# Last stage of a three-stage image kernel: the normalisation of one image pair woven into the MLP of the pair before it, written out instruction by instruction on every engine

## The chip, the cores and the metric

One NeuronCore of a Trainium2 chip runs the whole program. The metric is device time in microseconds (us). One NeuronCore has a tensor engine (PE in the profile, with its weight loads as PEld), a vector engine (DVE), a scalar engine (ACT), GpSimd (POOL) and a sync engine (SP) that here only issues DMAs. Each engine works through its own instructions in order, and semaphores tie the engines together.

## The reference, cut to what matters

Three stages follow one another: an attention block, a 25-step non-negative factorisation (which leaves `h`), and the stage that this change touches. That last stage is, for 32 images of 96 channels by 32 x 32 pixels:

```
def layernorm_last(x, g, b):
    mu = x.mean(axis=-1, keepdims=True)
    var = ((x - mu) ** 2).mean(axis=-1, keepdims=True)
    return (x - mu) * lax.rsqrt(var + 1e-05) * g + b
...
x = x + nnmf_conv(jnp.maximum(x_norm, EPS), Wc)      # nnmf_conv returns h
y = x.transpose(0, 2, 3, 1)
yn = layernorm_last(y, g2, b2)
hid = jax.nn.gelu(yn @ w_fc1 + b_fc1, approximate=False)
y = y + (hid @ w_fc2 + b_fc2)
return y.transpose(0, 3, 1, 2)
```

The normalisation is over the 96 channels; the MLP goes from 96 to 384 and back to 96.

## The kernel before

Only the last stage, `token_mlp`, matters here. Channels lie on the partitions. The work goes by pairs of images, 16 pairs in all, and each pair has four units (`UNITS = 4`) of 96 channels by 512 pixels. The buffers carry the prefix `ml_` in the profile.

**Normalisation of a pair (`norm`).** SP loads `xt` (2 DMAs) and `ht` (8 DMAs) one pair ahead. ACT copies `ht` into pixel order, four `hn` copies (L1433). DVE adds them, `yt` (L1503), once for each image. Then for each unit: PE subtracts the mean by a float32 product with `centre` (`ml_PX`, L1558); ACT squares it (`ml_sqr`, L1440); PE averages over the channels (`ml_PV`, L1551); ACT takes Ln (`ml_vl`, L1447) and Exp (`ml_vy`, L1451); DVE refines the inverse root and scales in four steps, `ml_va`, `ml_vb`, `ml_vr`, `ml_yn` (L1507, L1509, L1511, L1515); ACT writes the float16 upper part `y16[0]` (L1466), and POOL the lower part `y16[1]` (L1408). `ml_PX`, `ml_PV`, `ml_sqr`, `ml_vy` and `ml_yn` are rings of two.

**MLP of a pair (`mlp`).** For each unit and each of three groups `m` of 128 hidden rows: PE multiplies in three float16 passes (`ml_PG`, L1578); ACT takes the gelu into `g32[m]` (L1475); DVE casts it to float16 (`g16[0]`, L1530); POOL subtracts to get the lower part (`g16[1]`, L1417). Then PE multiplies back with nine passes (`ml_PO`, one buffer, L1569), DVE adds bias and `yt` into `ml_ot` (L1523), and SP stores it (L1390). `g32` has three buffers, one for each `m`.

**Order.** `program` runs the same coarse order on every engine: the whole normalisation of pair b+1, then the whole MLP of pair b, and so on; a hardware loop over t holds two pairs. No engine starts the MLP's instructions before it has issued all of its normalisation instructions. ACT loads another function table at the start of each half (L1425, L1475).

Of the kernel before, what the change touches and what calls it, by code (L numbers as in the profile page):

```python
# [1285 lines left out]
UNITS = 4  # L1286


def token_mlp(nc, x2_dram, h_dram, g2, be2, wf1, bf1, wf2, bf2, out):
# [9 lines left out]
    with ctx:  # L1299
# [64 lines left out]
        @block.sync
        def _(e):
# [16 lines left out]
            def norm(b, p, early):  # L1382

                if not (isinstance(b, int) and b == B - 1):
                    load(b + 1, 1 - p, isinstance(b, int) and b == 0)

            def mlp(b, p, early):
                for u in range(UNITS):
                    e.wait_ge(s_out, UNITS * b + u + 1)
                    e.dma_start(out[bass.ds(2 * b + u // 2, 1), :, HALF * (u % 2):HALF * (u % 2) + HALF].rearrange("a c n -> (a c) n"),  # L1390
                                ot[u % 2][:, :]).then_inc(s_stored[u % 2], 16)
            load(0, 0, True)
            program(e, norm, mlp)
            for v in (0, 1):
                e.wait_ge(s_stored[v], 16 * NIMG)
# [23 lines left out]

        @block.scalar  # L1420
        def _(e):
            e.wait_ge(s_ready, 1)

            def norm(b, p, early):
                e.preload_act_table_set("natural_log_exp_and_others")  # L1425
                for v in (0, 1):
                    i = 2 * p + v
                    e.wait_ge(s_h_loaded[p], 64 * (b - p) + 128)
                    if not (isinstance(b, int) and b == 0):
                        e.wait_ge(s_y, 2 * b + v - 1)  # L1430
                    for y in (0, 1):

                        e.activation(hn[v][:, :].rearrange("c (r y k x) -> c y r k x", y=2, k=AC, x=PX)[:, y],  # L1433
                                     ht[p][:, :, y, :, :, v].rearrange("c x k r -> c r k x"), ACT.Copy, scale=1.0 / H_SCALE).then_inc(s_hn, 1)
                def square(u):
                    n = UNITS * b + u
                    e.wait_ge(s_centred, n + 1)
                    if not (isinstance(b, int) and b == 0 and u < 2):
                        e.wait_ge(s_var, n - 1)
                    e.activation(sqr[u % 2][:, :], PX_[u % 2][0:CH, :], ACT.Square).then_inc(s_sqr, 1)  # L1440

                def inverse_root(u):
                    n = UNITS * b + u
                    e.wait_ge(s_var, n + 1)
                    if not (isinstance(b, int) and b == 0 and u < 1):
                        e.wait_ge(s_vy, n)
                    e.activation(vl[:, :], PV[u % 2][0:CH, :], ACT.Ln, bias=eps_c[:, :]).then_inc(s_vl, 1)  # L1447
                    e.wait_ge(s_vl, n + 1)
                    if not (isinstance(b, int) and b == 0 and u < 2):
                        e.wait_ge(s_vr, n - 1)  # L1450
                    e.activation(vy[u % 2][:, :], vl[:, :], ACT.Exp, scale=-0.5).then_inc(s_vy, 1)  # L1451


                square(0); square(1)
                for u in range(0, UNITS, 2):
                    inverse_root(u); inverse_root(u + 1)
                    for v in (u, u + 1):
                        high(b, p, v, early)
                        if v + 2 < UNITS:
                            square(v + 2)  # L1460

            def high(b, p, u, early):
                e.wait_ge(s_yn, UNITS * b + u + 1)
                if not early:
                    e.wait_ge(s_fc1, 3 * (UNITS * (b - 2) + u) + 3)
                e.activation(y16[0][:, p, u, :], yn[u % 2][:, :], ACT.Copy).then_inc(s_yn_hi, 1)  # L1466

            def mlp(b, p, early):
                for u in range(UNITS):
                    for m in range(3):  # L1470
                        n = 3 * (UNITS * b + u) + m
# [139 lines left out]
```

## Time and profile before

| | |
|---|---|
| three runs, median (lowest to highest) | 7554.52 us (7553.3 to 7556.19) |
| profiled execution, its own time | 7552.64 us |
| its span, first to last instruction | 7550.9 us |
| mean granted TensorE clock | 0.956 |
| last stage, from about 6757 us to the end | about 794 us |
| busy in six pairs of the last stage, mean per pair | PE 30.4, DVE 26.8, ACT 24.6, POOL 19.9 us of 47.8 |

The windows of pairs run from one second-half centring to the next. Rows of a view give the start or the busy time first, then the engine, the line and the operation, with outputs to the left of the arrow; what stands in brackets is how long the engine had been idle and what ended the wait.

### The profile page before, as it was taken

Reading aid. Unit: us, or ns where it says so; the run is one execution under the profiler, and the core shown is the slowest. Engines: PE = TensorE matmul, PEld = TensorE weight load, DVE = VectorE, ACT = ScalarE, POOL = GpSimd, SP = SyncE. Lnnn points to the kernel's source line nnn. Section 1 sums busy time; section 2 is a strip of 40 time slices with the busy share of each in tenths; the row PEclk is TensorE's granted clock in tenths of the full one; section 3 lists DMA queues with packets and bytes.
Section 4 is the critical chain, followed back from the end, with each engine's and each line's share of the span. In section 5 each row is a group of like instructions: output and inputs, shape, how many; then the busy total and the mean of one; then the engine's idle time right before and its main releaser. Section 6 shows DMA issues by size and latency. Waiting matters only on the chain. (4 is left out here: it accounts for less than half of the span.)

```text
span 7550.9 us, 237789 instructions
## 1 busy us (share of the span) xinstructions
PE 6477.1 (86%) x97977; PEld 3568.9 (47%) x97977; DVE 5483.5 (73%) x8000; ACT 4590.7 (61%) x6901; POOL 4709.7 (62%) x3220
## 2 busy tenths in 40 slices
PE   7999999999588888888888878888878888866666
PEld 3444444444355555455555545555545555532222
DVE  5666666666588888778888868888868888865555
ACT  3444444444277777667777757777757777755554
POOL 3333333333188788768888767888767888863444
PEclk9999999999799999999999999999999999987778
DMA  0000000000100000000000010000010000011111
GB/s 15 20 22 24 17 24 20 22 24 16 37 3 3 3 3 3 31 11 3 3 3 3 3 39 3 3 3 3 3 39 3 3 3 3 3 45 38 50 50 38
DMA packets 92369, 119.74 MB, mean 16 GB/s; under 512 B 23696, under 2 KB 73136, under 8 KB 91568
## 3 DMA queue, kind: packets, MB, share of 16 engines
q1 hardware_dynamic: 91568, 106.87, 4.7%
q8 instruction: 770, 12.62, 0.7%
q14 instruction: 31, 0.25, 0.0%
HBM read 53.67 MB, written 52.79 MB: 14 GB/s over the span
## 5 line engine op out<-in xcount | busy, mean ns | idle before, releaser
L190 POOL TENSOR_TENSOR nn_hf<-nn_hf,nn_sr 128x512 f32<-128x512 f32 (+1 forms) x800 | 1444.3, 1828 | 807.7 <-DVE nn_sr L380 807.7
L464 PE MATMUL nn_P<-nn_hh,nn_w 64*64 64x256 f16 x38400 | 1565.2, 279 | 319.2 <-issue 86.9
L464 PEld LDWEIGHTS nn_P<-nn_hh,nn_w 64*64 64x64 f16 x38400 | 980.7, 108 | 1001.7 <-issue 948.3
L385 DVE SCALAR_TENSOR_TENSOR nn_P<-nn_P,nn_xs 128x612 f32<-128x612 f32 x1200 | 962.3, 802 | 546.9 <-PE nn_P L464 537.1
L471 PE MATMUL nn_P<-nn_nh,nn_w 64*64 64x512 f16 x19200 | 1276.1, 379 | 72.1 <-DVE nn_hf L371 9.3
L258 ACT ACTIVATE nn_yy<-nn_P 128x612 f32<-128x612 f32 x1200 | 810.2, 675 | 787.2 <-DVE nn_P L385 782.4
L1168 PE MATMUL at_PC<-at_xp,at_w1T 97*128 97x512 f16 x5184 | 1235.8, 383 | 0.0
L391 DVE TENSOR_TENSOR nn_P<-nn_P,nn_nh 128x612 f32<-128x612 f32 x1200 | 958.2, 798 | 123.7 <-ACT nn_nh L262 116.3
L396 DVE SCALAR_TENSOR_TENSOR nn_nl<-nn_P,nn_yy 128x612 f16<-128x612 f32 x1200 | 952.0, 793 | 88.4 <-ACT nn_yy L265 56.2
L464 PE MATMUL nn_P<-nn_hl,nn_w 64*64 64x256 f16 x19200 | 988.3, 274 | 0.0
L276 ACT ACTIVATE nn_hh<-nn_hf 128x512 f16<-128x512 f32 (+1 forms) x780 | 650.8, 834 | 523.9 <-POOL nn_hf L190 523.8
L371 DVE TENSOR_TENSOR nn_hf<-nn_P,nn_hf 128x512 f32<-128x512 f32 x1200 | 786.9, 684 | 136.6 <-PE nn_P L471 136.6
L262 ACT ACTIVATE nn_nh<-nn_yy 128x612 f16<-128x612 f32 x1200 | 856.3, 714 | 37.9
L184 POOL TENSOR_TENSOR nn_acc<-nn_acc,nn_hf 128x512 f32<-128x512 f32 x600 | 768.7, 1281 | 125.0 <-DVE nn_hf L371 124.6
L265 ACT ACTIVATE nn_yy<-nn_yy 128x612 f32<-128x612 f32 x1200 | 836.6, 697 | 0.0
L202 POOL TENSOR_TENSOR nn_hl<-nn_hf,nn_hh 128x1024 f16<-128x1024 f32 x384 | 823.5, 2144 | 0.0
L471 PEld LDWEIGHTS nn_P<-nn_nh,nn_w 64*64 64x64 f16 x19200 | 532.3, 105 | 592.2 <-issue 366.7
L1168 PEld LDWEIGHTS at_PC<-at_xp,at_w1T 97*128 97x128 f16 x5184 | 495.1, 97 | 657.8 <-issue 89.4
L471 PE MATMUL nn_P<-nn_nl,nn_w 64*64 64x512 f16 x9600 | 743.2, 375 | 0.0
L464 PEld LDWEIGHTS nn_P<-nn_hl,nn_w 64*64 64x64 f16 x19200 | 590.8, 109 | 4.5 <-issue 0.8
L194 POOL TENSOR_TENSOR nn_hl<-nn_hf,nn_hh 128x512 f16<-128x512 f32 x392 | 458.8, 1170 | 0.0
L505 PE MATMUL nn_PS<-nn_acc,nn_blk 128*128 128x512 f32 x400 | 226.1, 647 | 260.1 <-POOL nn_acc L184 260.1
(210 smaller groups left out, 7742.0 us busy)
## 6 DMA issues: line engine op xcount, KB each, us to landing
xn_scratch<-at_xb SPq DMA_DIRECT2D x128, 114.8 KB
nn_xs<-xn_scratch SPq DMA_DIRECT2D x48, 306.0 KB, 4.5
at_x<-in_x SPq DMA_DIRECT2D x32, 384.0 KB, 3.2
x_scratch<-at_x SPq DMA_DIRECT2D x64, 192.0 KB, 2.1
h_scratch<-nn_hf SPq DMA_DIRECT2D x48, 256.0 KB, 2.8
ml_xt<-x_scratch SPq DMA_DIRECT2D x32, 384.0 KB, 4.7
ml_ht<-h_scratch SPq DMA_DIRECT2D x128, 96.0 KB
out<-ml_ot SPq DMA_DIRECT2D x64, 192.0 KB, 2.1
```

Source lines behind the costliest of these rows:

```text
L190: e.tensor_tensor(hf[c][:, g, :], hf[c][:, g, :], sr[:, :].unsqueeze(1).broadcast_to((128, g.stop - g.start, A_COLS)), ALU.mult).then_inc( ...
L202: e.tensor_tensor(hl[c][:, g, :], hf[c][:, g, :], hh[c][:, g, :], ALU.subtract).then_inc(h_lo_late, 1)
L258: e.activation(half(yy[k % RING][:, :]), Pv[k % 2], ACT.Ln).then_inc(logged, 1)
L262: e.activation(flat_nu(nh, k), yy[k % RING][:, :], ACT.Exp, scale=-1.0).then_inc(nu_hi, 1)
L265: e.activation(yy[k % RING][:, :], yy[k % RING][:, :], ACT.Exp, scale=-1.0).then_inc(inverted, 1)
L371: e.tensor_tensor(hf[c][:, g, :], P2[:, g % 2, :], hf[c][:, g, :], ALU.mult).then_inc(h_raw, 1)
L385: e.scalar_tensor_tensor(Pv[k % 2], Pv[k % 2], EPS * H_SCALE * W_SCALE, half(xs[u][:, k, :, :].rearrange("p i n -> p (i n)")), ALU.max, AL ...
L391: e.tensor_tensor(Pv[k % 2], Pv[k % 2], half(flat_nu(nh, k)), ALU.mult).then_inc(nu_back, 1)
L396: e.scalar_tensor_tensor(half(flat_nu(nl, k)), Pv[k % 2], 1.0, half(yy[k % RING][:, :]), ALU.subtract, ALU.mult, reverse0=True).then_inc(n ...
L464: return pe.matmul(out[:, 0:AC, rows_y] if near else out[:, 1:BC, rows_y], w1[rows, wp, a, 1 if near else 0, k, cols], (hh, hl)[dp][u][row ...
L471: return pe.matmul(P2[cols, g % 2, :], w2[rows, wp, a, 1 if near else 0, g, cols], src[:, :, 0:AC, :] if near else src[:, :, 1:BC, :], sta ...
L1168: mm = e.matmul(PC[u % 2][:, :], w1T[wp_][:, c, tap, :], xp[q][dp][:, 16 * h + dy:16 * h + dy + 16, dx:dx + HW], start=(tap, wp_, dp) == ( ...
```

## The change

Only `token_mlp` changes. The two coarse halves become single operations (`centring`, `variance`, `widen`, `narrow`, `residual`, `g_high` and so on, with the same arithmetic, shapes and counts as before), and each engine gets a `step` in which the operations of pair n (b0), pair n-1 (b1) and pair n-2 (b2) stand in an order written out by hand. `pairs` runs steps 0 to 17: four unrolled, ten in a hardware loop, four unrolled. The names map as follows: `residual` is `ml_yt`, `log_var` and `inv_root` are `ml_vl` and `ml_vy`, `y_high` and `y_low` are the parts of `ml_y`, `widen` is `ml_PG`, `gelu` fills `g32`, `g_high` and `g_low` are the parts of `ml_g`, `narrow` is `ml_PO` and `result` is `ml_ot`. The rings `sqr`, `vy`, `yn` and `ot` go from two to four, `g32` from three to six, `g16` from six to twelve slots. PSUM buffers stay as they are. Loads are issued two pairs ahead instead of one.

```diff
-        def program(e, norm, mlp):
-            norm(0, 0, True); norm(1, 1, True); mlp(0, 0, True)
-            norm(2, 0, False); mlp(1, 1, False)
-            with e.Fori(1, B // 2 - 1) as t:
-                norm(2 * t + 1, 1, False); mlp(2 * t, 0, False)
-                norm(2 * t + 2, 0, False); mlp(2 * t + 1, 1, False)
-            norm(B - 1, 1, False); mlp(B - 2, 0, False); mlp(B - 1, 1, False)
...
+        def pairs(e, step):
+            first = 4
+            for n in range(first):
+                step(n, n % 2, n // 2)
+            with e.Fori(first // 2, B // 2 - 1) as t:
+                step(2 * t, 0, t)
+                step(2 * t + 1, 1, t)
+            for n in range(B - 2, B + AHEAD):
+                step(n, n % 2, n // 2)
...
@@ SP
+            def step(n, p, t):
+                store(pair(n, p, t, 2), 3)
+                load((n + 2, p, t + 1)) if not isinstance(n, int) or n + 2 < B else None
+                store(pair(n, p, t, 1), 0)
+                store(pair(n, p, t, 1), 1)
+                store(pair(n, p, t, 1), 2)
...
@@ POOL
+                y_low(b0, 0); g_low(b1, 3, 0); y_low(b0, 1); g_low(b1, 3, 1); g_low(b1, 3, 2); y_low(b0, 2); g_low(b0, 0, 0)
+                g_low(b0, 0, 1); y_low(b0, 3); g_low(b0, 0, 2); g_low(b0, 1, 0); g_low(b0, 1, 1); g_low(b0, 1, 2)
+                g_low(b0, 2, 0); g_low(b0, 2, 1); g_low(b0, 2, 2)
...
@@ ACT
+            def gelu(b, p, t, u, m):
+                need(e, s_fc1, 3 * (UNITS * b + u) + m + 1)
+                need(e, s_g_lo, 3 * (UNITS * b + u) + m - 5)
...
+                norm_table(b1); log_var(b1, 0); inv_root(b1, 0); square(b1, 1); log_var(b1, 1); inv_root(b1, 1); y_high(b1, 0)
+                square(b1, 2); copy_h(b0, 0, 0); log_var(b1, 2); inv_root(b1, 2); square(b1, 3); y_high(b1, 1); log_var(b1, 3)
+                inv_root(b1, 3); gelu_table(b1); gelu(b1, 0, 0); y_high(b1, 2); gelu(b1, 0, 1); gelu(b1, 0, 2); gelu(b1, 1, 0)
+                copy_h(b0, 0, 1); gelu(b1, 1, 1); y_high(b1, 3); gelu(b1, 1, 2); copy_h(b0, 1, 0); gelu(b1, 2, 0)
+                copy_h(b0, 1, 1); gelu(b1, 2, 1); gelu(b1, 2, 2); square(b0, 0); gelu(b1, 3, 0); gelu(b1, 3, 1); gelu(b1, 3, 2)
...
@@ DVE
+                residual(b0, 0); g_high(b1, 1, 2); g_high(b1, 2, 0); result(b2, 3); g_high(b1, 2, 1); g_high(b1, 2, 2)
+                residual(b0, 1); g_high(b1, 3, 0); g_high(b1, 3, 1); result(b1, 0); var_a(b0, 0); var_b(b0, 0)
+                refine_root(b0, 0); scale(b0, 0); var_a(b0, 1); var_b(b0, 1); refine_root(b0, 1); scale(b0, 1); g_high(b1, 3, 2)
+                var_a(b0, 2); var_b(b0, 2); result(b1, 1); refine_root(b0, 2); var_a(b0, 3); scale(b0, 2); var_b(b0, 3)
+                g_high(b0, 0, 0); refine_root(b0, 3); g_high(b0, 0, 1); result(b1, 2); scale(b0, 3); g_high(b0, 0, 2)
+                g_high(b0, 1, 0); g_high(b0, 1, 1)
...
@@ PE
+            def widen(b, p, t, u, m):
+                need(e, s_yn_lo, UNITS * b + u + 1)
+                need(e, s_g, 3 * (UNITS * b + u) + m - 2)
...
+                centring(b0, 0); centring(b0, 1); widen(b1, 3, 1); widen(b1, 3, 2); variance(b0, 0); narrow(b1, 0)
+                variance(b0, 1); narrow(b1, 1); centring(b0, 2); variance(b0, 2); centring(b0, 3); variance(b0, 3)
+                widen(b0, 0, 0); narrow(b1, 2); widen(b0, 0, 1); widen(b0, 0, 2); widen(b0, 1, 0); widen(b0, 1, 1)
+                widen(b0, 1, 2); widen(b0, 2, 0); narrow(b1, 3); widen(b0, 2, 1); widen(b0, 2, 2); widen(b0, 3, 0)
```

DVE, in the main loop before: the refinement of two units and the start of the casts, with the register instructions (REGISTER_ALU, ISA) that carry the waits of a loop.

```order
L1507 SCALAR_TENSOR_TENSOR ml_va<-ml_PV,ml_vy 96x512
L1509 TENSOR_TENSOR ml_vb<-ml_va,ml_vy 96x512
L1511 SCALAR_TENSOR_TENSOR ml_vr<-ml_vb,ml_vy 96x512
L1514 REGISTER_ALU
L1515 SCALAR_TENSOR_TENSOR ml_yn<-ml_PX,ml_vr 96x512
```

DVE, in the main loop of the change, from the third unit's `ml_yn` on: the fourth unit's refinement of one pair stands between the casts of the first unit's gelus, and later the next pair's `ml_yt` between casts.

```order
L1541 SCALAR_TENSOR_TENSOR ml_yn<-ml_PX,ml_vr 96x512
L1377 REGISTER_ALU
L1529 TENSOR_TENSOR ml_vb<-ml_va,ml_vy 96x512
L1377 ISA
L1547 CAST ml_g_0<-ml_g_0 128x512
L1377 REGISTER_ALU
L1535 SCALAR_TENSOR_TENSOR ml_vr<-ml_vb,ml_vy 96x512
L1377 REGISTER_ALU
L1547 CAST ml_g_0<-ml_g_1 128x512
L1553 SCALAR_TENSOR_TENSOR ml_ot<-ml_PO,ml_bf2c,ml_yt 96x512
L1541 SCALAR_TENSOR_TENSOR ml_yn<-ml_PX,ml_vr 96x512
```

What moved is that casts, results and refinement now alternate, and almost every one of them has a register instruction ahead of it.

PE, in the main loop before: the start of a normalisation.

```order
L1558 MATMUL ml_PX<-ml_yt,ml_centre 96x512 x2
L1548 REGISTER_ALU
L1551 MATMUL ml_PV<-ml_sqr,ml_mean_w 96x512
L1548 REGISTER_ALU
L1551 MATMUL ml_PV<-ml_sqr,ml_mean_w 96x512
```

PE, in the main loop of the change, the same place.

```order
L1579 MATMUL ml_PX<-ml_yt,ml_centre 96x512 x2
L1377 ISA x2
L1592 MATMUL ml_PG<-ml_y_0,ml_w_0 128x512
L1592 MATMUL ml_PG<-ml_y_0,ml_w_1 128x512
L1592 MATMUL ml_PG<-ml_y_1,ml_w_0 128x512
L1592 MATMUL ml_PG<-ml_y_0,ml_w_0 128x512
L1592 MATMUL ml_PG<-ml_y_0,ml_w_1 128x512
L1592 MATMUL ml_PG<-ml_y_1,ml_w_0 128x512
L1377 REGISTER_ALU
L1377 ISA
L1585 MATMUL ml_PV<-ml_sqr,ml_mean_w 96x512
```

The last two `widen` of the pair before now stand behind both `centring` of the next pair, so they are behind whatever those wait for.

## Rows read from the trace of the kernel before

**Rows 1.** The page: the span.
```profile
span 7550.9 us, 237789 instructions
```

**Rows 2.** Windows of pairs: length, PE, PEld, DVE, ACT, POOL busy, PEclk.
```profile
7062.10:7110.58 48.48, 31.41 (x88) 11.88 (x88) 26.86 (x34) 24.55 (x34) 19.89 (x16) 0.78 0.17 49
...
sum 286.76, PE 182.53 PEld 69.19 DVE 160.88 ACT 147.28 POOL 119.14; mean PE 30.42 PEld 11.53 DVE 26.81 ACT 24.55 POOL 19.86
```

**Rows 3.** Groups by line, 6918.7 to 7445.45 us, eleven pairs: busy, mean ns.
```profile
L1417 POOL TENSOR_TENSOR ml_g<-ml_g,ml_g 128x512 f16<-128x512 f32 x88 | 108.9, 1256 | 4.0 <-DVE ml_g L1530 4.0
...
L1530 DVE CAST ml_g<-ml_g 128x512 f16<-128x512 f32 x132 | 95.7, 738 | 68.5 <-ACT ml_g L1475 67.8
L1475 ACT ACTIVATE ml_g<-ml_PG,ml_b 128x512 f32<-128x512 f32 x132 | 86.2, 686 | 82.8 <-PE ml_PG L1578 58.5 <-POOL ml_g L1417 24.2
...
L1433 ACT ACTIVATE ml_hn<-ml_ht 96x512 f32<-96x512 f32 x44 | 44.0, 1075 | 0.1
...
L1509 DVE TENSOR_TENSOR ml_vb<-ml_va,ml_vy 96x512 f32<-96x512 f32 x44 | 41.2, 935 | 1.5
...
L1503 DVE TENSOR_TENSOR ml_yt<-ml_hn,ml_xt 96x1024 f32<-96x1024 f32 x22 | 25.9, 1215 | 0.0
```

**Rows 4.** Timeline, one normalisation: start, duration, engine, instruction.
```profile
7050.86 1.95 PE L1558 MATMUL ml_PX<-ml_yt,ml_centre 96*96 96x512 f32 x4 [2.05 <-DVE ml_yt L1503]
...
7051.52 7.24 SPq L1379 DMA_DIRECT2D ml_ht<-h_scratch  x8
...
7052.07 0.59 ACT L1440 ACTIVATE ml_sqr<-ml_PX 96x512 f32<-96x512 f32 x1 [3.42 <-PE ml_PX L1558]
...
7053.85 0.68 ACT L1447 ACTIVATE ml_vl<-ml_PV,ml_eps_c 96x512 f32<-96x512 f32 x1 [0.41 <-PE ml_PV L1551]
...
7055.23 0.69 DVE L1507 SCALAR_TENSOR_TENSOR ml_va<-ml_PV,ml_vy 96x512 f32<-96x512 f32 x1 [3.36 <-ACT ml_vy L1451]
...
7055.95 0.69 DVE L1509 TENSOR_TENSOR ml_vb<-ml_va,ml_vy 96x512 f32<-96x512 f32 x1
...
7056.67 0.69 DVE L1511 SCALAR_TENSOR_TENSOR ml_vr<-ml_vb,ml_vy 96x512 f32<-96x512 f32 x1
7057.48 0.69 DVE L1515 SCALAR_TENSOR_TENSOR ml_yn<-ml_PX,ml_vr 96x512 f32<-96x512 f32 x1
...
7058.91 1.15 POOL L1408 TENSOR_TENSOR ml_y<-ml_yn,ml_y 96x512 f16<-96x512 f32 x1 [12.29 <-ACT ml_y L1466]
7058.92 1.68 DVE L1509 TENSOR_TENSOR ml_vb<-ml_va,ml_vy 96x512 f32<-96x512 f32 x1
...
7063.92 3.62 PE L1551 MATMUL ml_PV<-ml_sqr,ml_mean_w 96*96 96x512 f32 x4
...
7074.66 1.28 ACT L1475 ACT_TABLE_LOAD   x1
```

**Rows 5.** Timeline, PE passes and the result behind them.
```profile
7046.67 2.14 PE L1569 MATMUL ml_PO<-ml_g,ml_w 128*96 128x512 f16 x9 [1.90 <-POOL ml_g L1417]
7048.85 0.75 DVE L1523 SCALAR_TENSOR_TENSOR ml_ot<-ml_PO,ml_bf2c,ml_yt 96x512 f32<-96x512 f32 x1 [3.19 <-PE ml_PO L1569]
...
7076.70 4.02 PE L1578 MATMUL ml_PG<-ml_y,ml_w 96*128 96x512 f16 x9 [7.01 <-ACT ml_g L1475]
```

**Rows 6.** Timeline, DVE alone, then POOL alone.
```profile
7032.65 0.82 DVE L1530 CAST ml_g<-ml_g 128x512 f16<-128x512 f32 x1 [0.47 <-ACT ml_g L1475]
7033.94 0.82 DVE L1530 CAST ml_g<-ml_g 128x512 f16<-128x512 f32 x1 [0.47 <-ACT ml_g L1475]
...
7038.16 0.43 DVE L1530 CAST ml_g<-ml_g 128x512 f16<-128x512 f32 x1 [0.58 <-ACT ml_g L1475]
...
7034.45 1.33 POOL L1417 TENSOR_TENSOR ml_g<-ml_g 128x512 f16<-128x512 f32 x1
```

**Rows 7.** Timeline, the stage's first square and its last result.
```profile
6779.45 0.59 ACT L1440 ACTIVATE ml_sqr<-ml_PX 96x512 f32<-96x512 f32 x1 [1.55 <-PE ml_PX L1558]
...
7547.58 0.75 DVE L1523 SCALAR_TENSOR_TENSOR ml_ot<-ml_PO,ml_bf2c,ml_yt 96x512 f32<-96x512 f32 x1 [3.29 <-PE ml_PO L1569]
```

More of the change, by code:

```diff
@@ L1380, in load, with store @@
                                 h_dram[bass.ds(b, 1), :, GC * j:GC * j + GC, :].rearrange("a g c n -> (a g) c n")).then_inc(s_h_loaded[p], 16)
[L1382 to L1395, printed above, removed]
+            @only
+            def store(b, p, t, u):
+                need(e, s_out, UNITS * b + u + 1)
+                e.dma_start(out[bass.ds(2 * b + u // 2, 1), :, HALF * (u % 2):HALF * (u % 2) + HALF].rearrange("a c n -> (a c) n"),
+                            ot[u][:, :]).then_inc(s_stored[u], 16)
+            def step(n, p, t):
[4 more added lines that the diff above has]
+                store(pair(n, p, t, 1), 2)
+            load((0, 0, 0))
+            load((1, 1, 0))
+            pairs(e, step)
+            for u in range(UNITS):
+                e.wait_ge(s_stored[u], 16 * B)
         @block.gpsimd
@@ L1422, in _, with norm_table @@
             e.wait_ge(s_ready, 1)
-            def norm(b, p, early):
+            @only
+            def norm_table(b, p, t):
                 e.preload_act_table_set("natural_log_exp_and_others")
[L1426 to L1471, printed above, removed]
-                        e.wait_ge(s_fc1, n + 1)
-                        if not early or u >= 1:
-                            e.wait_ge(s_g_lo, n - 2)
-                        e.activation(g32[m][:, :], PG[m][:, :], ACT.Gelu, bias=b1[:, m:m + 1]).then_inc(s_g, 1)
@@ L1476, in _, with gelu_table, copy_h @@
-            program(e, norm, mlp)
+            @only
+            def gelu_table(b, p, t):
+                e.preload_act_table_set("gelu_and_others")
+            @only
+            def copy_h(b, p, t, v, y):
+                need(e, s_h_loaded[p], 128 * (t + 1))
+                need(e, s_y, 2 * b + v - 1)
+                e.activation(hn[v][:, :].rearrange("c (r y k x) -> c y r k x", y=2, k=AC, x=PX)[:, y],
+                             ht[p][:, :, y, :, :, v].rearrange("c x k r -> c r k x"), ACT.Copy, scale=1.0 / H_SCALE).then_inc(s_hn, 1)
@@ new lines, in inv_root, with y_high @@
+            @only
+            def inv_root(b, p, t, u):
+                need(e, s_vl, UNITS * b + u + 1)
+                need(e, s_vr, UNITS * b + u - 3)
+                e.activation(vy[u][:, :], vl[:, :], ACT.Exp, scale=-0.5).then_inc(s_vy, 1)
+            @only
+            def y_high(b, p, t, u):
+                need(e, s_yn, UNITS * b + u + 1)
+                need(e, s_fc1, 3 * (UNITS * (b - 2) + u) + 3)
+                e.activation(y16[0][:, p, u, :], yn[u][:, :], ACT.Copy).then_inc(s_yn_hi, 1)
@@ L1478, in _ @@
+            pairs(e, step)
         @block.vector
@@ L1536, in _ @@
+            pairs(e, step)
         @block.tensor
@@ L1582, in _, with centring, variance @@
-            program(e, norm, mlp)
+            @only
+            def centring(b, p, t, u):
+                need(e, s_y, 2 * b + u // 2 + 1)
+                need(e, s_yn, UNITS * b + u - 1)
+                e.matmul(PX_[u % 2][0:CH, :], centre[:, :], yt[2 * p + u // 2][:, HALF * (u % 2):HALF * (u % 2) + HALF], start=True, stop=True).then_inc(s_centred, 1)
+            @only
+            def variance(b, p, t, u):
+                need(e, s_sqr, UNITS * b + u + 1)
+                need(e, s_vab, 2 * (UNITS * b + u) - 3)
+                e.matmul(PV[u % 2][0:CH, :], mean_w[:, :], sqr[u][:, :], start=True, stop=True).then_inc(s_var, 1)
@@ L1584 @@
+            pairs(e, step)
 _INS = ['x'] + ['L0_conv_' + n for n in ('wq', 'sq', 'bq', 'wkv', 'skv', 'bkv', 'wp', 'sp', 'bp', 'w1', 's1', 'b1', 'wdw', 'bdw', 'w2', 's2', 'b2')] \
```

203 lines of the change are left out of this document (100 added, 103 removed).

## The prediction

> **What bounds the kernel now.** I read four views, from coarse to fine. The page gives the span [rows 1]. The windows of six pairs in the last stage say that a pair takes 286.76/6 = 47.8 us, while the busiest engine by work that can't overlap itself, DVE, has 26.8 us, ACT 24.6 and POOL 19.9 [rows 2]. PE shows 30.4, but its granted clock is 0.78 in the window printed, so part of that is passes at the low level. No engine is full: about 21 us of each pair is waiting. The timeline of one normalisation shows why [rows 4]. Only one chain runs: centring, square, variance, logarithm and exponential, four DVE steps, and nothing of the MLP is issued beside it, since `program` puts the whole normalisation ahead of the whole MLP on every engine. From the first centring at 7050.86 to the gelu table load at 7074.66 pass 23.8 us, and the MLP with the next `hn` copies takes the other 24. So the bound is latency in two serial halves, not an engine. PE idles, its clock falls to 1.2 GHz, and nine passes then take 4.02 us where they take 2.14 at 2.4 GHz [rows 5].
>
> **What the change does to it.** Counts and shapes of all arithmetic stay. What changes is which instructions stand beside each other, so the sum is a new length for one pair, times the pairs. I follow one pair in the main loop by the written orders. T = 0 is the start of the logarithm table load on ACT. "Next" is the pair behind it.
>
> *Part A, T = 0 to the exponential of unit 3.* ACT: table 1.28 (the last of [rows 4]); logarithm and exponential of unit 0, 1.38 (7053.85 to 7055.23), so 2.7. `square(1)` 0.63, 3.3. `variance(1)` to its logarithm is 1.19 (7052.66 to 7053.85), 4.5, and the pair of activations gives 5.9. `centring(2)` would be free at 5.7, when `scale(0)` ends (four steps of about 0.75 from 2.7), but on PE it is queued behind `narrow(b1, 1)`, 2.14 us after `variance(1)`, so it begins at 6.3. Centring to square is 1.21 (7050.86 to 7052.07), 7.5; square 0.63, 8.1; variance 1.19, 9.3 (one `copy_h` of 1.08 [rows 3] fits in); activations 1.38, 10.7; `square(3)` 0.63, 11.3; variance 1.19, 12.5; activations, 13.9. Before, the same four units took 23.8 from the first centring with their `ml_y`. Part A holds at the full clock.
>
> *Part B, DVE from there to `residual(next, 1)`.* First `var_a(3)` and `scale(2)`, 0.72 each, to 15.3. Then sixteen instructions: `var_b(3)` and `refine_root(3)`, nine `g_high`, two `result`, `scale(3)` and two `residual`. Ten POOL subtractions want to run in the same stretch. What they cost each other is the unknown. The row of a cast alone is 0.43 and beside a running subtraction 0.82, and casts follow each other every 1.29 us [rows 6]; the mean over the loop is 0.74 [rows 3]. An `ml_vb` that starts with a POOL subtraction takes 1.68 and not 0.69: it waits 0.99 of POOL's 1.15 [rows 4]. POOL is busy 20 of 47.8 us before, but about two thirds of the MLP half, where the casts lie; in part B it would be somewhat denser. So I take 0.78 for a cast (just over its mean), 1.1 for `var_b` and `refine_root` (between 0.69 and 1.68, near the mean 0.94 of `ml_vb`), and 1.6 for a residual (1.22 alone, plus less than half a wait). Results stay at 0.75 and `scale` at 0.69, since these read PSUM and no row shows them stretched. A register instruction now stands before nearly every DVE instruction of the loop. Where one stands in the kernel before, between `ml_vr` and `ml_yn`, the second starts 0.81 after the first and not 0.72 (7056.67 and 7057.48 against 7055.23 and 7055.95 [rows 4]). With some of them hidden in waits I take 0.08 a step for gap and register. Sum: 9 x 0.78 + 2 x 1.1 + 2 x 1.6 + 2 x 0.75 + 0.7 + 16 x 0.08 = 15.9, to 31.2.
> Bounds: with no contention and 0.03 gaps, 9 x 0.43 + 2 x 0.69 + 2 x 1.22 + 1.5 + 0.7 + 0.5 = 10.4; with the ten subtractions each holding DVE off for 0.99, 10.4 + 9.9 = 20.3 less what overlaps the results, about 19.8.
>
> On that wait the Trainium skill ("SBUF — State Buffer", section "Who interferes with whom") says that a DVE instruction with two SBUF inputs, or a cast in a two-port mode, and a GpSimd one share a port that is an exclusive lock for the whole instruction. The 1.68 us of `ml_vb` agrees with a full block. Taken strictly it would put part B at the upper bound, 19.8 us instead of my 15.9, and a pair at 38.4; but the casts' 1.29 us spacing beside a POOL subtraction of 1.33 [rows 6] shows that a part of each POOL instruction does not keep DVE out, and DVE often waits for a gelu anyway. The lock taken in full is a rival below.
>
> *Part C, the return to ACT.* `widen(3, 1)` and `widen(3, 2)` are queued on PE behind `centring(next, 1)`, which needs that residual. Before, they waited only for work of their own pair. Centring 1.21, three passes 0.7 (a third of 2.14), two gelus 2 x 0.69 [rows 3]: 3.3, to 34.5. Queued behind that wait on PE are the two widens, both variances and two narrows; ACT waits for the widens. That ACT is late there and not at the bound shows by its own load: after 13.9 it has a table load, ten gelus, three copies, two `y_high` and a square, 1.28 + 6.9 + 3.2 + 1.3 + 0.6 = 13.3, to 27.2; it then waits for part C. The g32 ring of six removes the wait of a gelu for POOL (24.2 us in eleven pairs [rows 3]).
>
> *Costed at nothing.* The copies of `h` between the gelus: ACT has room; if it had none they would cost the 3.2 us. The loads: SP still issues ten DMAs a pair, 7.24 us for the eight of `ht` [rows 4], with stores behind them; a store late by 8 us meets a ring of four `ot`, so no result waits for it before the next pair. The loads are two pairs ahead, over 60 us. SBUF size costs nothing.
>
> **The sum.** The first table load comes after the first square, 6779.45 + 0.63 = 6780.1 [rows 7], as before. Fifteen pairs at 34.5 are 517.5, so the last pair's T = 0 is at 7297.6. In it no next pair holds ACT up and POOL ends last: `y_low(2)` to 17.7, then thirteen subtractions every 1.29 to 34.5, then narrow 2.18 (7046.67 to 7048.85 [rows 5]), result 0.75 and 2.6 from there to the span's end (7548.33 to 7550.9): 40.0. The span is 7337.6 against 7550.9, 213 us less. The profiled execution's own time was 7552.64, 1.7 over its span, and the median of the three runs is 1.9 above that: 7341 us, -2.8%.
>
> **The rivals.**
> *The engines meet less than I say* (part B near 10.4 to 14): for it, casts that find POOL idle take 0.43 and POOL has only 20 us of work; against it, the mean of 0.74. A pair of 29 to 33, at 31: 15 x 3.5 = 52 us less, 7289. Chance 0.23.
> *The low clock stays in the normalisation part.* Two float32 products take 3.62 us there and 1.95 at the full clock [rows 4]. Part A has four products and a narrow on its path: 4 x 0.83 + 1.9 = 5.2 more, a pair of up to 39.7; half of it is a pair of 37.1 and 7380. For it: the clock fell before with PE idle for a few us between centrings. Against: PE now has narrows and widens in between, 8 x 2.14 + 4 x 1.95 = 24.9 of 34.5 us. Chance 0.15.
> *The lock in full*, a pair of 38.4, 15 x 3.9 = 58 more: 7400. Chance 0.11.
> *Slower than before.* If PE ran all of the stage at 1.2 GHz, a pair would need 8 x 4.02 + 4 x 3.62 = 46.6 us of PE alone. With over 1.2 us of idle time a pair it passes 47.8, and with the 5 us that its in-order waits for `residual` and `scale` cost, 51.6: 7555 + 15 x 3.8 = 7610. It decides when the clock falls for the whole pair; against it stands that it was granted 0.78 at far less work. Chance 0.02, and 0.01 that nothing measurable changes, because some ring or queue serialises the halves again.
>
> **How the numbers follow.** My case is a pair of 33 to 36.3, 7318 to 7368, chance 0.48. The range takes it whole and reaches into both neighbours: 7283 to 7405 leaves out about 0.09 below and 0.09 above. A measurement of this kernel tells 0.2%, 15 us, from no change, which is one us a pair. Faster 0.97, same 0.01, slower 0.02.
>
> **What would show it.** In the windows, a pair of 33 to 36 us and a granted clock over 0.9. In the groups, casts at 0.75 to 0.85 us and `ml_vb` over 0.94. In the waits, ACT `ml_g` waiting for PE `ml_PG` in the fourth unit, behind `ml_PX`, by 3 to 6 us a pair; if that wait is missing, part C is wrong. A pair at 29 to 31 with ACT nearly full makes the contention term wrong; a clock near 0.8 or float32 products of 1.8 us makes the clock rival right.

## The result, and the profile after

The changed kernel takes 7315.9 us (median of 4 runs, 7313.29 to 7318.79), the kernel before beside it 7553.91 (4 runs): a ratio of 0.9685, interval 0.9674 to 0.9697, so 238 us less. The prediction was 7341, with 7283 to 7405 as its range: the sign, the size and the range hold, and the point is 25 us too long. The parts from which that point was made fit less well than their sum.

The windows of the kernel after give one early and one middle pair, from logarithm table load to logarithm table load, and then ten pairs of the hardware loop in one window (length, PE, PEld, DVE, ACT, POOL busy, PEclk).

```profile
6879.14:6912.13 32.99, 27.02 (x94) 11.30 (x95) 31.38 (x38) 23.43 (x34) 23.00 (x17) 0.95 0.27 78
7006.85:7038.31 31.46, 24.86 (x88) 10.40 (x87) 29.07 (x35) 23.48 (x35) 23.25 (x17) 0.95 0.26 75
6879.14:7200.28 321.14, 262.79 (x889) 108.14 (x889) 296.47 (x344) 236.47 (x340) 229.97 (x161) 0.92 0.25 74
```

A pair takes 321.14/10 = 32.1 us where it took 47.8 [rows 2]. DVE is now busy 29.6 of them, 92%, though its arithmetic is the same as when it showed 26.8 [rows 2]: busy time holds what an instruction waits for inside itself. The groups by line from 6879.14 to 7231 (eleven pairs less 2 us) say where that is.

```profile
L1427 POOL TENSOR_TENSOR ml_g<-ml_g,ml_g 128x512 f16<-128x512 f32 x109 | 161.2, 1496 | 4.8 <-DVE ml_g L1547 4.8
L1547 DVE CAST ml_g<-ml_g 128x512 f16<-128x512 f32 x134 | 116.8, 904 | 4.8 <-ACT ml_g L1483 4.8
...
L1483 ACT ACTIVATE ml_g<-ml_PG,ml_b 128x512 f32<-128x512 f32 x130 | 86.4, 681 | 18.5 <-POOL ml_g L1427 11.6 <-PE ml_PG L1592 6.5
...
L1517 DVE TENSOR_TENSOR ml_yt<-ml_hn,ml_xt 96x1024 f32<-96x1024 f32 x22 | 46.9, 2131 | 0.1
L1535 DVE SCALAR_TENSOR_TENSOR ml_vr<-ml_vb,ml_vy 96x512 f32<-96x512 f32 x44 | 45.5, 1033 | 0.9
...
L1529 DVE TENSOR_TENSOR ml_vb<-ml_va,ml_vy 96x512 f32<-96x512 f32 x44 | 39.5, 897 | 1.4
...
L1553 DVE SCALAR_TENSOR_TENSOR ml_ot<-ml_PO,ml_bf2c,ml_yt 96x512 f32<-96x512 f32 x45 | 33.2, 737 | 0.0
...
L1523 DVE SCALAR_TENSOR_TENSOR ml_va<-ml_PV,ml_vy 96x512 f32<-96x512 f32 x44 | 30.0, 681 | 17.7 <-ACT ml_vy L1471 17.4
```

Two more groups of the kernel before, from the view of [rows 3]:

```profile
L1523 DVE SCALAR_TENSOR_TENSOR ml_ot<-ml_PO,ml_bf2c,ml_yt 96x512 f32<-96x512 f32 x44 | 32.9, 747 | 62.8 <-PE ml_PO L1569 62.8
...
L1507 DVE SCALAR_TENSOR_TENSOR ml_va<-ml_PV,ml_vy 96x512 f32<-96x512 f32 x44 | 30.2, 687 | 95.0 <-ACT ml_vy L1451 94.2
```

Against [rows 3] the cast goes from 738 to 904 ns, `ml_yt` from 1215 to 2131, POOL's subtraction from 1256 to 1496. `ml_ot`, which reads PSUM, stays at its 0.75. DVE's idle time falls in three places: in front of `ml_va` from 95.0 us in eleven pairs to 17.7, of the casts from 68.5 to 4.8, of the results `ml_ot` from 62.8 to 0.0. That is 18.5 us a pair, of which 2.8 come back as longer DVE instructions: this is where the 16 us a pair came from.

### The profile page after: what moved, and what is told of

Its sections match the earlier page's. It is cut to its first block and busy times, and to the rows that moved or that the text cites. A ratio compares the mean times of both kernels' runs of the same rounds, so it can differ in the third digit from the quotient of the medians.

```text
span 7311.5 us, 237584 instructions
## 1 busy us (share of the span) xinstructions
PE 6411.8 (88%) x97977; PEld 3552.4 (49%) x97977; DVE 5529.1 (76%) x8000; ACT 4575.9 (63%) x6902; POOL 4757.4 (65%) x3220
```

## The experiments

In all of them "a pair" is the mean distance of logarithm table loads over ten loop pairs, part A runs from that load to the gelu table load and part B from there to the next pair. The changed kernel has 32.1 = 16.2 + 15.9. The stage's first table load lies between 6775 and 6791 us in the traces of the changed kernel and its variants, whatever was edited behind it, so totals that differ by less than some 10 us are not told apart, and the pairs are the finer measure.

The granted clock between 6900 and 7200 moves with these changes too. It is 0.92 in the changed kernel, 1.00 with POOL's subtractions short and 0.94 unrolled; it is 0.85 with `g32` as a ring of three, 0.87 with the casts on ACT, 0.82 with `residual` on POOL, 0.89 with short casts, 0.85 with the copies together, 0.85 with the narrow moved and 0.90 with it moved and unrolled. A lower clock can follow from a longer wait or be part of what it costs, and no run here separates the two.

**Order or rings?** The changed kernel's rings and early loads, with each engine's old coarse order:

```diff
-  y_low(b0, 0); g_low(b1, 3, 0); y_low(b0, 1); g_low(b1, 3, 1); ...
+  for u in range(UNITS): y_low(b0, u)
+  for u in range(UNITS):
+      for m in range(3): g_low(b1, u, m)      # and ACT, DVE, PE, SP likewise
```

> The changed kernel's rings, operations and loads two pairs ahead, but every engine in the old coarse order: a whole normalisation, then the whole MLP of the pair before. Theory 'interleaving': a pair stays at 44 to 47 us and the time at 7490 to 7555. Rival 'rings': after the run with three g32 buffers lost 77 us of the gain of 238, the rings may carry most of it: 7320 to 7420.

Measured: 7555.2 us, ratio 1.0003 (0.9994 to 1.0012). Larger rings alone give nothing; all of the gain needs the interleaved order.

**The order with g32 as a ring of three**, all else as in the change:

```diff
-  g32 = [... for i in range(6)];  need(e, s_g_lo, 3 * (UNITS * b + u) + m - 5)
+  g32 = [... for i in range(3)];  need(e, s_g_lo, 3 * (UNITS * b + u) + m - 2)
```

> The changed kernel with g32 a ring of three again, each gelu waiting for the POOL subtraction three back instead of six. Theory 'port' (DVE is full because DVE and POOL hold each other off; ACT has 8 us of slack a pair): 0 to 1 us a pair more, 7316 to 7331. Rival 'rings': the wait of before, 24.2 us in eleven pairs, comes back doubled on a schedule that has no room, 2 to 4 us a pair, 7346 to 7376.

Measured: 7392.62, ratio 0.9788 (0.9772 to 0.9805), a pair of 37.3 = 16.0 + 21.3. Two rows of the waits of this kernel between 6900 and 7200 (engine and line, what it waited for, us in total, times, longest):

```profile
ACT ml_g L1483 <- POOL ml_g L1427: 38.8, 22, 3.5
PE ml_PG L1592 <- ACT ml_g L1483: 31.7, 21, 3.3
```

So 77 of the 238 us hang on this ring, more than either theory gave it: a gelu waits for POOL up to 3.5 us, and all of the loss is in part B, where the gelus are. In [rows 3] that wait was 24.2 us in eleven pairs; with the order interleaved and the ring unchanged it is 38.8 in eight. A wait that was small becomes the next bound when the large one goes.

**What POOL costs.** POOL's subtractions run over 32 columns instead of 512, in the changed kernel and in the kernel before. The lower parts of `y16` and `g16` are left out for the other columns.

```diff
-  e.tensor_tensor(g16[1][:, 3 * u + m, :], g32[...][:, :], g16[0][:, 3 * u + m, :], ALU.subtract)
+  e.tensor_tensor(g16[1][:, 3 * u + m, 0:32], g32[...][:, 0:32], g16[0][:, 3 * u + m, 0:32], ALU.subtract)
```

> The changed kernel with every POOL subtraction of the last stage cut from 512 to 32 columns (the lower float16 parts are left out of the result for the rest, zeros are multiplied in their place); counts, order and waits stay. Theory 'port': casts fall from 0.90 to about 0.45 us, residuals from 2.13 to 1.22, DVE's busy time a pair from 31 to about 22 us, and the pair to 26.5 to 28.5 us, where ACT and the chain bound it: 7235 to 7265. Rival 'chain' (the order of the queues and the latencies between the engines set the pair, contention only fills DVE's waiting): the pair stays over 30.5 us, 7290 or more.

> The kernel before with the same cut of the POOL subtractions. It says what POOL cost the old order. In the MLP half casts wait 0.3 us each and the last subtractions stand on the way to the PE; in the normalisation one DVE step in eight waits 1 us. I expect 5 to 8 us a pair less, 7430 to 7475. If POOL had cost the old order nothing, 7550; if the port had been the bound there too, under 7400.

Measured: the changed kernel with it 7229.23, ratio 0.9567 (0.9551 to 0.9583), a pair of 26.9 = 13.7 + 13.2; the kernel before with it 7494.68, ratio 0.9923 (0.9906 to 0.9939), a pair of 44.4. Window and groups of the changed kernel with short subtractions, 6900 to 7200:

```profile
6900.00:7200.00 300.00, 264.61 (x977) 109.68 (x975) 226.79 (x381) 257.65 (x380) 76.69 (x178) 1.00 0.26 78
```

```profile
L1548 DVE CAST ml_g<-ml_g 128x512 f16<-128x512 f32 x133 | 55.9, 432 | 18.3 <-ACT ml_g L1483 15.5
...
L1530 DVE TENSOR_TENSOR ml_vb<-ml_va,ml_vy 96x512 f32<-96x512 f32 x45 | 31.9, 709 | 1.5
...
L1518 DVE TENSOR_TENSOR ml_yt<-ml_hn,ml_xt 96x1024 f32<-96x1024 f32 x22 | 26.8, 1216 | 1.3 <-issue 1.3
```

The cast is back at 0.43 and `ml_yt` at 1.22, with their own work untouched. So the difference to 0.90 and 2.13 is what POOL's full subtractions add: 12 x 0.47 + 2 x 0.91 + 4 x (0.19 + 0.35) = 9.6 us of DVE's 29.6 a pair (29.6 - 20.4 = 9.2 by the windows). The clock is granted in full and ACT is at 86%; in one part B (6961.88 to 6975.04) ACT is busy for 12.95 of 13.16 us, so this bare order is at ACT's load there, 13.3 as the prediction added it up. (PE shows 13.15 in the same stretch, but its ends are modelled, and the gelus wait for it only 1.8 us between 6900 and 7200.) Of a pair's 32.1 us, 5.2 are what POOL's subtractions cost in all: what they add to DVE's instructions, POOL's own time on the way to the gelus and narrows, and what the clock gives back when they are gone; the run does not split these. In the kernel before they cost 3.4 (47.8 less 44.4), less than was expected. That a chain of waits stays there when they are gone is the likely reason; it was not tested.

**Can the cost be moved away?** Three attempts, with the full work in the first two. The middle cast of each unit on ACT:

```diff
+  def g_high_act(b, p, t, u):   # behind gelu(b, u, 2) on ACT; DVE's g_high(b, u, 1) goes
+      e.activation(g16[0][:, 3 * u + 1, :], g32[3 * (u % 2) + 1][:, :], ACT.Copy)
```

> The changed kernel with the middle cast of each unit (g_high of m = 1, four of twelve a pair) moved from DVE to ACT, behind the third gelu of its unit, with a semaphore of its own. Theory 'port' (DVE with its waits for POOL is the bound, ACT has 8 us idle a pair): DVE loses 4 x 0.90 us, ACT gains 4 x 0.65, the pair goes from 32.1 to 28.5 to 30.5 us: 7262 to 7292. Rival 'order' (the ring of g32 and POOL's in-order subtractions bind at the gelus): a later cast on ACT delays POOL and the gelus of the unit after next, no gain or a loss, 7310 to 7350.

Measured: 7321.07, ratio 0.9693 (0.968 to 0.9706), a pair of 33.3 = 16.7 + 16.6. This is inside the rival's range. Groups of this kernel, 6900 to 7200:

```profile
L1557 DVE CAST ml_g<-ml_g 128x512 f16<-128x512 f32 x72 | 58.8, 819 | 25.6 <-ACT ml_g L1493 24.2
...
L1487 ACT ACTIVATE ml_g<-ml_g 128x512 f16<-128x512 f32 x36 | 23.0, 640 | 0.0
```

DVE now waits for gelus. ACT's slack (it is busy 23.6 of 32.1) lies mostly in part A; in part B it has 13.3 of work, and four casts of 0.64 make it 15.9. Part A grew as well, by 0.5, where none of these casts stands; that share is not explained.

`residual` on POOL:

```diff
-  DVE:  residual(b0, 0); ... residual(b0, 1)
+  POOL: g_low(b0, 1, 1); residual(a, 0); g_low(b0, 1, 2) ... g_low(b0, 2, 2); residual(a, 1)
```

> The changed kernel with both additions of h and x of a pair (residual) on POOL instead of DVE, behind the subtractions that they stood beside. DVE loses 2 x 2.13 us a pair, POOL gains about 2 x 2.3 and goes to 27 of 32. If it is DVE's own occupancy that sets the second part: 1.5 to 2.5 us a pair less, 7278 to 7294. If DVE and POOL share one resource that is full there, moving work from one to the other brings nothing, and POOL's queue delays centring: 7312 to 7350.

Measured: 7400.24, ratio 0.9802 (0.9788 to 0.9815), a pair of 38.5 = 16.3 + 22.1, worse than both theories. `ml_yt` takes 2.51 us on POOL, and the next pair's start hangs on it. The wait of DVE for gelus, and that of PE for `ml_yt` (6900 to 7200); that the gelus come late in consequence is my reading of the order:

```profile
DVE ml_g L1548 <- ACT ml_g L1491: 71.5, 46, 5.7
...
PE ml_PX L1580 <- POOL ml_yt L1424: 38.4, 8, 4.9
```

DVE's casts over 32 columns (the upper part of `g16` is left out for the others):

```diff
-  e.tensor_copy(g16[0][:, 3 * u + m, :], g32[3 * (u % 2) + m][:, :])
+  e.tensor_copy(g16[0][:, 3 * u + m, 0:32], g32[3 * (u % 2) + m][:, 0:32])
```

> The changed kernel with the DVE casts g_high cut from 512 to 32 columns (the upper float16 part of the gelus is left out for the rest, zeros stand in its place); POOL's subtractions keep their full length, ACT and PE their work. Theory 'mutual' (DVE's casts hold POOL off as POOL holds DVE off): POOL's subtraction of ml_g falls from 1.50 to under 1.30 us though nothing of it is changed, the residual falls under 2 us, and the pair to 28 to 30 us: 7245 to 7290. Rival 'POOL alone' (POOL's in-order queue with its own work is the bound in the second part): its instructions keep about 1.45 us and the pair stays over 31 us, 7295 or more.

Measured: 7300.95, ratio 0.9665 (0.9648 to 0.9681), a pair of 31.9 = 16.6 + 15.3. Two groups and one wait of this kernel, 6900 to 7200:

```profile
L1427 POOL TENSOR_TENSOR ml_g<-ml_g,ml_g 128x512 f16<-128x512 f32 x93 | 117.7, 1284 | 3.4 <-DVE ml_g L1548 3.2
...
L1548 DVE CAST ml_g<-ml_g 128x32 f16<-128x32 f32 x111 | 44.9, 427 | 22.1 <-ACT ml_g L1483 21.8
```

```profile
PE ml_PV L1586 <- ACT ml_sqr L1459: 35.8, 29, 3.0
```

The durations go as mutual holding off says: most of POOL's subtractions fall from 1.50 to 1.28 (the others stay at 1.52), `ml_yt` from 2.13 to 1.94, and a cast of 32 columns, 0.18 where it runs free, takes 0.43 in the mean. The time hardly follows: a pair stays at 31.9, and the 15 us in the total are 0.2%. DVE is busy 24.5 us a pair instead of 29.6, so its 92% were no proof that DVE's load set the pair. What holds it now was not shown. DVE waits more for the exponentials (`ml_va`, 34.9 us between 6900 and 7200, where the changed kernel, measured again below, has 16.6), `ml_vb` takes 1.11 and not 0.90, and the clock is 0.89 and not 0.92: a loop of waits through PE and ACT, in which `ml_vb`, `ml_vr` and `ml_yt` still wait for POOL, would look like this.

**Register instructions?** All pairs unrolled instead of ten in a hardware loop, the order the same:

```diff
-  with e.Fori(first // 2, B // 2 - 1) as t: step(2 * t, 0, t); step(2 * t + 1, 1, t)
+  for n in range(B + AHEAD): step(n, n % 2, n // 2)
```

> The changed kernel with all 18 steps written out, no hardware loop, so no register instruction ahead of the waits; order and work are the same. If the register instructions cost their 0.08 to 0.12 us a step on DVE, which is full 97% of the pair, ten pairs lose about 1.5 to 3 us each: 7286 to 7302. Rival: they are hidden in the waits for POOL's share of the port, 7312 to 7320 as the changed kernel (7316).

Measured: 7303.28, ratio 0.9673 (0.966 to 0.9686), and from the fourth on each pair is 30.7 = 15.1 + 15.7, where the loop's vary from 30.4 to 33.0. `ml_vb` takes 0.69 and not 0.90: with each pair spaced alike it meets no subtraction. DVE's busy time falls from 29.6 us a pair (92%, not the 97% of the expectation) to 28.4, and what is left between its instructions only from 2.5 to 2.4. So most of the 1.4 us are shorter meetings with POOL and not gaps saved, and starts 0.79 and 0.80 us apart occur here as well (`ml_va`, `ml_vb` and `ml_vr` at 6958.89, 6959.68, 6952.21 and 6953.01), with no register instruction in the order. A cost of the register instructions as such is thus not shown. The 1.4 us a pair are in the trace; the intervals of the two ratios overlap, so as a total it isn't told apart from the changed kernel. It is the lowest median with all work done.

**The four copies of `h` in one place**, between the gelus of units 1 and 2:

```diff
-  copy_h(b0, 0, 0) after square(b1, 2); copy_h(b0, 0, 1), copy_h(b0, 1, 0), copy_h(b0, 1, 1) between later gelus
+  gelu(b1, 1, 2); copy_h(b0, 0, 0); copy_h(b0, 0, 1); copy_h(b0, 1, 0); copy_h(b0, 1, 1); gelu(b1, 2, 0)
```

> The changed kernel with the four copies of h of a pair in one block behind the gelus of unit 1, instead of one in the normalisation part and three between gelus. ACT has slack, but gelus stall for 4.4 us behind the block and DVE's casts with them. If ACT's slack covers it: 7312 to 7325. If the spacing between the gelus matters, since DVE and POOL are full there and then run dry, 1 to 3 us a pair more: 7330 to 7365.

Measured: 7361.75, ratio 0.9751 (0.9736 to 0.9766), a pair of 35.1 = 16.4 + 18.7. The spacing is worth 46 us. Two rows of ACT's timeline show the block, and what stands behind it:

```profile
7017.77 4.01 ACT L1452 ACTIVATE ml_hn<-ml_ht 96x512 f32<-96x512 f32 x4
...
7025.70 0.59 ACT L1459 ACTIVATE ml_sqr<-ml_PX 96x512 f32<-96x512 f32 x1 [2.19 <-PE ml_PX L1579]
```

The gelus wait 4 us for the copies, DVE waits for `ml_hn` (16.4 us in seven waits between 6900 and 7200), and the next pair's first square comes late.

**A filler taken out of PE's gap.** Part A was longer than forecast, and `narrow(b1, 1)` stands in it ahead of `centring(b0, 2)`. It is moved up, in the loop and with the pairs unrolled, beside another measurement of the changed kernel. `result(b1, 0)` on DVE goes up with it, since the narrow needs the one buffer `ml_PO` free; the two moves were not run apart.

```diff
-  variance(b0, 0); narrow(b1, 0); variance(b0, 1); narrow(b1, 1); centring(b0, 2)
+  variance(b0, 0); narrow(b1, 0); narrow(b1, 1); variance(b0, 1); centring(b0, 2)
-  residual(b0, 1); g_high(b1, 3, 0); g_high(b1, 3, 1); result(b1, 0)        # DVE
+  residual(b0, 1); result(b1, 0); g_high(b1, 3, 0); g_high(b1, 3, 1)
```

> The changed kernel as it is, on the same chip as the next three, for differences of less than 1%. Every theory: 7308 to 7324.

> The changed kernel with two moves: on DVE result(b1, 0) goes ahead of the two casts of unit 3, and on PE narrow(b1, 1) ahead of variance(b0, 1), where PE was idle 3 us and its clock fell, so that centring(b0, 2) no longer stands behind it. Theory 'chain in the first part' (my part A is a chain of latencies with narrow(b1, 1) on it): centring(2) 1.3 us earlier and at the full clock, a pair 1.3 to 1.8 us shorter, 7286 to 7298. Rival 'port only': the chain moves, but the DVE is as full as before, and two casts come 0.7 us later: 7308 to 7324.

> The same two moves and all 18 steps written out without a hardware loop. If the register instructions cost the 1.4 us a pair that the unrolled kernel's trace shows (30.7 against 32.1 us) and the moves 1.3 to 1.8, they add up: 7270 to 7288. If both only shorten the same wait: 7290 to 7300.

Measured: the changed kernel again 7316.93, 0.9687 (0.9673 to 0.97), a pair of 32.2; moved 7329.1, 0.97 (0.9687 to 0.9713), a pair of 33.7 = 18.0 + 15.8; moved and unrolled 7313.74, 0.9682 (0.9668 to 0.9695), 32.0. Two things are in the trace with the narrow moved up. The first is the clock; PE's timeline:

```profile
6994.08 1.09 PE L1585 MATMUL ml_PV<-ml_sqr,ml_mean_w 96*96 96x512 f32 x2
6997.00 1.07 PE L1579 MATMUL ml_PX<-ml_yt,ml_centre 96*96 96x512 f32 x2 [1.83 <-DVE ml_yn L1541]
6998.91 1.36 PE L1585 MATMUL ml_PV<-ml_sqr,ml_mean_w 96*96 96x512 f32 x2 [0.84 <-ACT ml_sqr L1459]
7000.69 1.99 PE L1579 MATMUL ml_PX<-ml_yt,ml_centre 96*96 96x512 f32 x2 [0.42 <-DVE ml_yn L1541]
7003.44 2.01 PE L1585 MATMUL ml_PV<-ml_sqr,ml_mean_w 96*96 96x512 f32 x2 [0.76 <-ACT ml_sqr L1459]
...
7006.53 3.75 PE L1601 MATMUL ml_PO<-ml_g,ml_w 128*96 128x512 f16 x9
```

Without the narrow in between, five products with idle time around them follow each other, the third takes 1.36 us and the fourth and fifth 2.0 instead of 1.0 (1.2 GHz and not 2.4), and the narrow behind them is slow as well (3.75 and not 2.11). The granted clock between 6900 and 7200 is 0.85 here, 0.93 in the changed kernel beside it. This is the prediction's clock rival in small, made by my own edit.

Yet this pair's part A is 16.1 us, no longer than the changed kernel's mean. The long pairs, of 36.4 us with a part A of 20.0, show the second thing:

```profile
6926.24 2.11 PE L1601 MATMUL ml_PO<-ml_g,ml_w 128*96 128x512 f16 x9 [1.83 <-DVE ml_ot L1553]
6928.19 1.02 PE L1585 MATMUL ml_PV<-ml_sqr,ml_mean_w 96*96 96x512 f32 x2
...
6929.31 0.68 ACT L1465 ACTIVATE ml_vl<-ml_PV,ml_eps_c 96x512 f32<-96x512 f32 x1 [4.21 <-PE ml_PV L1585]
```

`variance(b0, 1)` now stands behind a narrow that itself waits 1.83 us for `result(b1, 0)`, and the logarithm waits 4.21 us. Between 6900 and 7200 ACT waits 44.3 us for `ml_PV`, where it waits 26.0 in the changed kernel beside it, some 2 us a pair. So the edit lost by its new place in the queue as well as by the clock, and the runs don't split the two. The unrolled kernel loses about the same by it, 32.0 against 30.7, and its pairs vary from 30.2 to 36.2 without any loop.

## Why the prediction was right or wrong, by its steps

**The bound, two serial halves of latency: right.** The coarse order with the new rings is the kernel before to 0.1%; the interleaved order removes the waits, and with `g32` left as a ring of three it keeps 161 of the 238 us.

**Part A, forecast 13.9, measured 16.2.** The timeline of ACT in the pair at T = 7006.85:

```profile
7006.85 1.28 ACT L1442 ACT_TABLE_LOAD   x1
...
7011.37 0.68 ACT L1465 ACTIVATE ml_vl<-ml_PV,ml_eps_c 96x512 f32<-96x512 f32 x1 [1.32 <-PE ml_PV L1585]
...
7015.88 0.59 ACT L1459 ACTIVATE ml_sqr<-ml_PX 96x512 f32<-96x512 f32 x1 [1.81 <-PE ml_PX L1579]
...
7017.80 0.68 ACT L1465 ACTIVATE ml_vl<-ml_PV,ml_eps_c 96x512 f32<-96x512 f32 x1 [0.32 <-PE ml_PV L1585]
...
7020.94 0.68 ACT L1465 ACTIVATE ml_vl<-ml_PV,ml_eps_c 96x512 f32<-96x512 f32 x1 [0.80 <-PE ml_PV L1585]
...
7022.31 1.28 ACT L1446 ACT_TABLE_LOAD   x1
```

And PE in the same place:

```profile
7010.18 1.09 PE L1585 MATMUL ml_PV<-ml_sqr,ml_mean_w 96*96 96x512 f32 x2 [3.01 <-ACT ml_sqr L1459]
7011.11 3.64 PE L1601 MATMUL ml_PO<-ml_g,ml_w 128*96 128x512 f16 x9
7014.55 1.22 PE L1579 MATMUL ml_PX<-ml_yt,ml_centre 96*96 96x512 f32 x2
```

The forecast had the second logarithm at T + 4.5, and it is at 4.5; the square of unit 2 at 7.5, and it is at 9.0; from there on all is 1.5 late, to 15.5 for the table load. The 1.5 us are one term: `narrow(b1, 1)` was taken at 2.14, but PE comes out of 3.01 us of idle time and the nine passes take 3.64, at 1.2 GHz for most of it. "Part A holds at the full clock" is what failed in this pair; other pairs add 0.7 in the mean, which the runs don't split between POOL's hold on `ml_vb` and `ml_vr` and the clock (with POOL short, part A is 13.7 at a clock of 1.00, and both are gone together).

**Part B, the contention term: mis-sized.** The forecast had a cast at 0.78, `ml_vb` and `ml_vr` at 1.1, a residual at 1.6. Measured: 0.90, 0.90 and 1.03, 2.13. Nine casts and two residuals are 9 x 0.12 + 2 x 0.53 = 2.1 us more, two refinements 0.3 less. The 0.08 us a step for gaps and registers, 1.3 in all, were not there either: in this stretch an instruction starts up to 0.08 before the recorded end of the one ahead (`ml_vb` at 7023.62 takes 1.42, and the cast behind it starts at 7024.96). In the pair shown the stretch from the last exponential (7022.29) to the end of the second `ml_yt` (7037.78 + 2.17 = 7039.95, rows below) takes 17.7 us against 17.3 forecast. Each size was off, and that their sum was not is luck.

The Trainium skill ("SBUF — State Buffer", section "Who interferes with whom") has the loser block fully, for the whole instruction of the other, in both directions, and no contention for an instruction with at most one SBUF input outside the two-port modes. The groups agree on the directions and on who is spared: POOL's 1.50 falls to 1.28 when casts are short, the cast's 0.90 to 0.43 when subtractions are, and `ml_ot`, with PSUM as its other input, stays at 0.74. Means can't show whether a single block is full. The pair that the lock in full was forecast to give, 38.4, did not come: its stretch up to the second `ml_yt` would have been 21.2 (1.4 + 19.8) and was 17.7, and the path on which that was to lie is that of the next step.

**Part C, "`centring(next, 1)`, which needs that residual": wrong, and the step that failed.** Units 0 and 1 both belong to image 0, so both centrings need only `residual(next, 0)`. DVE, PE and ACT of the changed kernel at the end of this pair:

```profile
7030.49 2.17 DVE L1517 TENSOR_TENSOR ml_yt<-ml_hn,ml_xt 96x1024 f32<-96x1024 f32 x1
7032.59 2.67 DVE L1547 CAST ml_g<-ml_g 128x512 f16<-128x512 f32 x2
...
7037.78 2.17 DVE L1517 TENSOR_TENSOR ml_yt<-ml_hn,ml_xt 96x1024 f32<-96x1024 f32 x1
```

```profile
7033.10 1.89 PE L1579 MATMUL ml_PX<-ml_yt,ml_centre 96*96 96x512 f32 x4
7034.83 1.46 PE L1592 MATMUL ml_PG<-ml_y,ml_w 96*128 96x512 f16 x6
```

```profile
7037.60 0.69 ACT L1483 ACTIVATE ml_g<-ml_PG,ml_b 128x512 f32<-128x512 f32 x1 [0.61 <-POOL ml_g L1427]
7038.31 1.28 ACT L1442 ACT_TABLE_LOAD   x1
```

Both centrings start 0.44 us after the first `ml_yt`, six passes of the widens stand right behind, and the next pair's table load comes 1.6 us before the second `ml_yt` has even ended. The sign that I had named (a wait of `ml_g` for `ml_PG` of 3 to 6 us a pair) is 6.5 us in eleven pairs. By my path this pair would have been 15.4 + 17.7 + 3.3 = 36.4 us; it is 31.5. The wrong dependency thus made the forecast about 5 us a pair too long, the narrow at half the clock and the rest of part A made it 2.3 too short, and so, by luck, 34.5 came out near 32.1. With POOL short the second half of the pair is 13.2 us, which is ACT's load of 13.3; in the changed kernel it is 15.9, 2.7 above that.

**The sum.** The stage begins 2.2 late (6782.28 against 6780.1), fifteen pairs take 482.6 and not 517.5, so 34.9 less, and the last pair with its tail takes 46.6 and not 40.0: 26 less together, 7311.5 against 7337.6. In the tail I had POOL end last, at 34.5 after T = 0, and one narrow behind it. POOL ends at 7297.08 + 5.96 = 7303.04, at 38.2, and the last pair's results follow each other through the single `ml_PO`:

```profile
7297.08 5.96 POOL L1427 TENSOR_TENSOR ml_g<-ml_g,ml_g 128x512 f16<-128x512 f32 x5
...
7298.20 3.80 PE L1601 MATMUL ml_PO<-ml_g,ml_w 128*96 128x512 f16 x9 [2.59 <-DVE ml_ot L1553]
...
7302.04 0.75 DVE L1553 SCALAR_TENSOR_TENSOR ml_ot<-ml_PO,ml_bf2c,ml_yt 96x512 f32<-96x512 f32 x1 [3.35 <-PE ml_PO L1601]
7305.08 0.75 DVE L1553 SCALAR_TENSOR_TENSOR ml_ot<-ml_PO,ml_bf2c,ml_yt 96x512 f32<-96x512 f32 x1 [2.30 <-PE ml_PO L1601]
7308.13 0.75 DVE L1553 SCALAR_TENSOR_TENSOR ml_ot<-ml_PO,ml_bf2c,ml_yt 96x512 f32<-96x512 f32 x1 [2.30 <-PE ml_PO L1601]
```

5.8 us lie between POOL's end and that of the last result, not 2.9, and POOL itself is 3.7 later than forecast: together the 6.6. The last narrow starts 2.9 us after POOL's end, so what it waits for is not POOL but the result ahead of it; the first of these three narrows runs at the low clock, 3.80 us for nine passes behind 2.59 of idle time.

**The rivals.** A pair of 32.1 lies outside my own case, 33 to 36.3, and inside the first rival's 29 to 33, but not by its mechanism: the engines meet more than forecast, not less. The clock rival holds for one narrow a pair, and for more of part A where the filler was moved. The lock in full was too dear even for the stretch that it was to lengthen. "Costed at nothing" holds for the loads, by the trace alone, since no run changed them; the copies cost nothing only where they stand apart (46 us together), and the ring of six was worth 77 us, far more than the 24.2 us of wait in eleven pairs from which it was costed.

**Open.** How part A's excess splits between the clock and POOL's hold; why the pairs of the loop vary between 30 and 34 us (with the narrow moved 31.8 to 36.4) while the unrolled ones don't, though with the narrow moved those do too (30.2 to 36.2), and the loop's don't with POOL's subtractions short (26.7 to 27.1); what the other rings and the early loads are worth one at a time; and whether the unrolled version is faster as a total. A narrow at the full clock without another filler was not tried.

## What to carry to other kernels

When two serial halves are interleaved, write for each wait which buffer's which part it needs, down to the image, before putting it on a path: one wrong dependency here was worth 5 us a pair, as much as POOL's subtractions cost in all. Size what two engines cost each other from the densest stretch of the trace, not from the mean, and look for the slack of the engine that is to help in the part of the period where it would be used. Before an instruction is moved, look at what it waits for, since all behind it in the queue will wait for that too, and whether it was what kept the clock up in a gap.
